# Two cross-attention blocks on one core: DMA queue entries placed by their producers, staging by chunks of heads, another order in the prologue and three banks at the end

## What is computed

```python
h1 = _ln(x, n1_g, n1_b)
x = _attn(h1, h1, q1, k1, v1, o1_w, o1_b, heads) + x
h2 = _ln(x, n2_g, n2_b)
x = _attn(h2, context, q2, k2, v2, o2_w, o2_b, heads) + x
h3 = _ln(x, n3_g, n3_b)
a, g = jnp.split(h3 @ ff_w1 + ff_b1, 2, axis=-1)
x = a * jax.nn.gelu(g, approximate=False) @ ff_w2 + ff_b2 + x
# _attn: softmax(q k^T / 4) v per head, then @ wo + bo
```

## Time and profile before

| what | value |
|---|---|
| median of three runs | 3865.36 us (3864.6 to 3879.61) |
| the profiled execution's own time | 3857.31 us |
| its span | 3855.5 us |
| mean granted TensorE clock | 0.914 of full speed |
| PE busy | 3224.7 us, 84% |
| weight loads (PEld) | 1495.8 us, 39% |
| DVE busy | 2090.1 us, 54% |
| ACT busy | 1996.1 us, 52% |
| POOL busy | 624.3 us, 16% |
| DMA engines, mean share of queue q1 | 33.7% |

### The profile page before, as it was taken

One profiled execution on the slowest core, in us unless ns is written; L12 is line 12 of the kernel. 1 busy time (PEld: TensorE's weight loads), 2 busy tenths in 40 slices (PEclk: granted clock), 3 DMA queues, 4 the chain that ended last, 5 costly groups with the idle time before them and its releaser, 6 DMA issues.

```text
span 3855.5 us, 43782 instructions
## 1 busy us (share of the span) xinstructions
PE 3224.7 (84%) x16320; PEld 1495.8 (39%) x16320; DVE 2090.1 (54%) x2565; ACT 1996.1 (52%) x3816; POOL 624.3 (16%) x676
## 2 busy tenths in 40 slices
PE   3686788899789878989889887898989979887867
PEld 1233343334344433534345332444334534533334
DVE  2554565667546655567546655555756645455410
ACT  1353366556555555556554565555655556454521
POOL 2113121212202121021201132021210031001010
PEclk9798898889899988999889998999989989998979
DMA  2642335431433344332333445333333133222202
GB/s 72 159 133 60 81 87 139 113 92 43 120 94 86 81 96 114 78 104 65 109 92 78 114 111 144 94 92 84 87 100 82 44 84 103 59 40 51 65 17 68
DMA packets 194323, 340.88 MB, mean 88 GB/s; under 512 B 19192, under 2 KB 101504, under 8 KB 192832
## 3 DMA queue, kind: packets, MB, share of 16 engines
q1 hardware_dynamic: 194112, 338.08, 33.7%
HBM read 202.29 MB, written 114.75 MB: 82 GB/s over the span
## 4 chain that ended last, share of the span: by engine, by line
PE 62%; DMA 11%; DVE 9%; ACT 6%; SPq 5%; issue 4%; POOL 3%; ACTq 0%; DVEq 0%; POOLq 0%
PE po L1053 12%; PE pr L1038 12%; PE pd L1019 8%; DVE mx L854 7%; DMA QS<-scr_q 6%; PE pf L969 5%; PE pf L977 5%; PE pf L916 4%; PE pf L957 3%; PE pf L939 3%; PE pf L948 3%; ACT ET L779 3%; DMA scr_k<-HS 2%; SPq L513 2%; PE pf L972 2%
## 5 line engine op out<-in xcount | busy, mean ns | idle before, releaser
L779 ACT ACTIVATE ET<-pr 128x512 f32<-128x512 f32 (+1 forms) x2720 | 1478.4, 597 | 1418.5 <-PE pr L1038 1406.0
L854 DVE TENSOR_REDUCE mx<-pd 128x2 f32<-128x804 f32 (+2 forms) x1600 | 1582.7, 1032 | 1056.2 <-PE pd L1019 1052.7
L1038 PE MATMUL pr<-QS,KS 64*128 64x512 f32 (+1 forms) x2720 | 877.1, 514 | 80.4 <-ACT ET L779 77.9
L1019 PE MATMUL pd<-KS,QS 64*128 64x400 f32 (+2 forms) x3200 | 636.4, 396 | 308.3 <-DMA QS<-scr_q 200.8
L1053 PE MATMUL po<-ET,V 128*32 128x512 f32 (+2 forms) x5440 | 779.9, 648 | 0.8 <-issue 0.6
L1038 PEld LDWEIGHTS pr<-QS,KS 64*128 64x128 f32 (+1 forms) x2720 | 345.3, 188 | 948.4 <-ACT ET L779 638.1
L1019 PEld LDWEIGHTS pd<-KS,QS 64*128 64x128 f32 x3200 | 374.4, 200 | 422.8 <-DMA QS<-scr_q 213.5
L673 POOL TENSOR_TENSOR HS<-uT,HS 128x512 fp32r<-128x512 f32 (+2 forms) x168 | 190.0, 1131 | 737.6 <-ACT uT L744 737.6
L969 PE MATMUL pf<-HS,WS 128*128 128x512 f32 x800 | 241.1, 433 | 72.2 <-DVE uT L847 24.9
L689 POOL TENSOR_TENSOR OA<-OA,DEN 128x512 f32<-128x512 f32 (+1 forms) x48 | 60.9, 1269 | 1311.4 <-DVE DEN L862 1311.4
L862 DVE RECIPROCAL DEN<-DEN 128x128 f32<-128x128 f32 (+1 forms) x192 | 170.5, 922 | 104.4 <-DMA DEN<-OU 103.7
(11 more groups left out here) (63 smaller groups left out, 2174.7 us busy)
## 6 DMA issues: line engine op xcount, KB each, us to landing
WS<-parts SPq DMA_DIRECT2D x160, 320.0 KB, 2.9
KS<-scr_k SPq DMA_DIRECT2D x80, 600.8 KB, 10.3
QS<-scr_q SPq DMA_DIRECT2D x80, 512.0 KB, 10.6
scr_k<-HS SPq DMA_DIRECT2D x144, 200.0 KB
scr_q<-HS SPq DMA_DIRECT2D x96, 256.0 KB
KS<-scr_k SPq DMA_DIRECT2D x80, 192.0 KB, 3.6
scr_k<-HS SPq DMA_DIRECT2D x48, 256.0 KB
OA<-OU SPq DMA_DIRECT2D x320, 32.0 KB
```

The lines of the kernel that those rows point to most:

```text
L779: activation(ET[0:q.rows[k], s % 2, 2 * pair + e, :], pr[e][0:q.rows[k], :], ACT.Exp).then_inc(score_free, 1)
L854: v.reduce_max(mx[:, t, 2 * p:2 * p + 2, c], pd[no % 2][:, :, 0:cols], AX_X).then_inc(unit_free, 1)
L1019: ins = mm(pd[no % 2][:, e, 0:cols], queries[:, t * P:(t + 1) * P], keys, start=True, stop=True)
L1038: mm(pr[e][0:m, :], keys, queries, start=True, stop=True).then_inc(score_ready, 1)
```

## The change

- **SP.** `beside` is split in three: loads behind a fill stand 2 beats behind it (`LOAD`), stores behind a split 4 (`STORE`), the bias row 8 (`LOAD_ROW`). `move_rows` stands 8 beats behind a group's end instead of 6; inverts at 14 to 17 instead of 13 to 19, the multiplication at 18 instead of 20.
- **Staging.** `stage_group` waits only for the last store of the chunk of heads that its group reads (`split_for`); k2's jobs go chunk of heads by chunk. The first unit stands from `_at + 7` instead of `_at + 5`.
- **Prologue.** `BEFORE` holds only chunk 0 of q1 and k1; chunks 1 and 2 (four fills) go to beats 1 to 9. DVE's memsets of KS stand behind the first measure. k2 of pass 0 and q1, k1 of pass 2 are spread over later beats; v1 is placed and waited for tile by tile.
- **Phases.** Two v2a fills go ahead of t3, and four a fills instead of three go with gelu.
- **Layer norm.** POOL adds the four bias rows behind the last tile instead of one behind each.
- **End.** From o2 of pass 7 on, fills take turns in three banks (pf, pr0, pr1); n3 measures a tile as soon as its o2 is in; g is written with Gelu at once; X is stored by tiles.

```diff
+KEY_JOBS = [(c, n, cols) for c in range(KC) for n, cols in CHUNKS]
-        seq = (mixed(places("tc", 0), places("n1", 1)) + places("t1", 1) + places("q1", 1) + places("k1", 1)
-               + places("k2", 0))
+        seq = [p for f in range(1, KC) for p in (("q1", 0, f), ("k1", 0, f))]
+        seq += mixed(places("tc", 0, 0, 3), places("n1", 1)) + places("t1", 1)
+        seq += [p for f in range(KC) for p in (("q1", 1, f), ("k1", 1, f))]
+        seq += places("tc", 0, 3) + places("k2", 0, 0, len(CHUNKS))
...
+        behind = places("v2a", c + 1)
         if c:
-            first, rest = gate(c - 1, 3)
-            seq += places("t3", c - 1) + places("g", c - 1) + [first] + rest
-        behind = places("v2a", c + 1)
+            first, rest = gate(c - 1, 4)
+            seq += behind[:2] + places("t3", c - 1) + places("g", c - 1) + [first] + rest
+            behind = behind[2:]
...
-BEFORE = places("n1", 0) + places("t1", 0) + places("q1", 0) + places("k1", 0) + places("v1", 0)
+BEFORE = places("n1", 0) + places("t1", 0) + [("q1", 0, 0), ("k1", 0, 0)] + places("v1", 0)
...
-COPY, MOVE, INVERT, DIVIDE = 5, 6, (13, 15, 17, 19), 20
+COPY, MOVE, INVERT, DIVIDE = 5, 8, (14, 15, 16, 17), 18
+LOAD, STORE, LOAD_ROW = 2, 4, 8
...
-    _at = max(4 * _host.end if _host else FIRST_BEAT, _stored + 1 if _stored >= 0 else FIRST_BEAT)
+    _at = max(4 * _host.end if _host else FIRST_BEAT, _stored + STORE + 1 if _stored >= 0 else FIRST_BEAT)
-    _from = max(_at + 5, _free, 0)
+    _from = max(_at + 7, _free, 0)
...
-                for own, count in stored_through(max(SPLIT[k, q.i, STAGE[k] - 1] + 1 for k in kinds)):
+                for own, count in stored_through(SPLIT[split_for(q)] + 1):
                     sp.wait_ge(own, count)
...
-                for p in PLACES.get(beat, []):
-                    beside(*p)
+                for p in PLACES.get(beat - LOAD, []) if beat - LOAD >= 0 else []:
+                    loads_behind(*p)
+                for p in PLACES.get(beat - STORE, []) if beat - STORE >= 0 else []:
+                    stores_behind(*p)
+                for p in PLACES.get(beat - LOAD_ROW, []) if beat - LOAD_ROW >= 0 else []:
+                    row_behind(*p)
                 for q in STAGE_AT.get(beat, []):
                     stage_group(q)
...
-                pool.wait_ge(w_in["b"], LOADED["b", stage, i])
-                pool.wait_ge(norm_done, at + 1)
-                gp.tensor_tensor(X[:, b, t, :], X[:, b, t, :], brow[:, :], ALU.add).then_inc(bias_done, 1)
+                if t == TT - 1:
+                    pool.wait_ge(w_in["b"], LOADED["b", stage, i])
+                    pool.wait_ge(norm_done, at + 1)
+                    for k in range(TT):
+                        gp.tensor_tensor(X[:, b, k, :], X[:, b, k, :], brow[:, :], ALU.add).then_inc(bias_done, 1)
...
+        def bank(no):
+            return pf if no < TAIL else (pf, pr[0], pr[1])[(no - TAIL) % len(tail_free)]
...
                 if beat == FIRST_BEAT:
+                    set_key_rows()
                     for u in range(len(GROUPS[0].units)):
```

More of the change, by code:

```diff
@@ L246, with split_for @@
             _user = _p
+TAIL = FILL["o2", N - 1, 0]
+def split_for(q):
+    own = [("q" if x == "q" else "k") + ("1" if q.kind == "S" else "2") for x in "qk"]
+    fills = [(own[0], q.i, q.g // 2)]
+    if q.kind == "S":
+        fills.append((own[1], q.i, q.g // 2))
+    else:
+        fills.append((own[1], q.i, len(CHUNKS) * (q.g // 2 + 1) - 1))
+    return max(fills, key=lambda p: SPLIT[p])
 STAGE_AT, UNITS_AT, TURN_AT, = {}, [0] * BEATS, {}
@@ L413, in blocks_kernel @@
         fill_free = sem("fill_free")
+        tail_free = [sem(f"tail_free{i}") for i in range(3)]
         low_done = sem("low_done")
@@ L533, in beside, with stores_behind @@
                         load_chunk(cc)
+                if stage in ("g", "a") and chunk_no(stage, i, f) + 2 < (i + 1) * 2 * FM:
+                    load_chunk(chunk_no(stage, i, f) + 2)
+                if stage not in LN_STAGES:
+                    for which, what, l in LOAD_BEHIND.get((stage, i, f), []):
+                        sp.wait_ge(fill_ready, FILL[stage, i, f] + 1)
+                        load_weights(which, what, l)
+                if stage == "tc" and f == STAGE[stage] - 1 and i < 2:
+                    sp.wait_ge(fill_ready, filled(stage, i))
+                    load_context(i + 1)
+                if stage == "ff2":
+                    if f == TT - 1 and i + 3 < N:
+                        sp.wait_ge(fill_ready, filled(stage, i))
+                        load_context(i + 3)
+                    if i // B == L - 1:
+                        for own, count in freed_through(FILL[stage, i, f]):
+                            sp.wait_ge(own, count)
+                        sp.dma_start(out[i % B, f * P:(f + 1) * P, :], X[:, i % B, f, :]).then_inc(x_stored, 16)
+            def stores_behind(stage, i, f):
                 if stage in ("q1", "k1", "q2", "k2"):
                     store_split(stage, i, f)
-                if stage in ("g", "a") and chunk_no(stage, i, f) + 2 < (i + 1) * 2 * FM:
-                    load_chunk(chunk_no(stage, i, f) + 2)
                 if stage == "w" and f:
@@ L541, in beside, with row_behind @@
                     load_raw(i, f)
-                for which, what, l in LOAD_BEHIND.get((stage, i, f), []):
-                    if which == "b":
+            def row_behind(stage, i, f):
+                if stage in LN_STAGES:
+                    for which, what, l in LOAD_BEHIND.get((stage, i, f), []):
                         sp.wait_ge(bias_done, TT * (LN0[stage, i] + 1))
[L545 to L555, removed]
-                        sp.wait_ge(fill_free, filled(stage, i))
-                        sp.dma_start(out[i % B].rearrange("(t p) d -> p t d", p=P), X[:, i % B, :, :]
-                                     ).then_inc(x_stored, 16)
+                        load_weights(which, what, l)
             def stage_group(q):
@@ L825, in measure @@
                         dve.wait_ge(fill_free, filled("ff2", i - B))
-                elif t == 0:
-                    dve.wait_ge(fill_free, filled("o1" if stage == "n2" else "o2", i))
+                elif stage != "n1":
+                    for own, count in freed_through(FILL["o1" if stage == "n2" else "o2", i, t]):
+                        dve.wait_ge(own, count)
                 v.bn_stats(stats[:, t, :], X[:, b, t, :]).then_inc(stats_done, 1)
```

144 lines of the change are left out of this document (91 added, 53 removed).

## The result

The changed kernel took 3684.7 us, median of 4 runs (3679.0 to 3690.2), beside 3865.0 us for the kernel before: a ratio of 0.953, 95% interval 0.950 to 0.956. So it is faster by 4.5%, where 6.5% was forecast. The time lies in the range of 3515 to 3700, 73 us above the forecast; the profiled execution stands at 3690.1.

The account below looks back on a forecast made before the run. PE was taken to set the pace but to be stopped often, above all by staging. 3857.3 - 47.9 + 11.2 - 193 - 23 = 3604.6, plus 8.1 for the runs, said as 3612 us; range 3515 to 3700.

Parts of the forecast that it names:

- Prologue, -48: Before the first unit: DVE's first measure ahead of the memsets, bias rows later, four fills out; 47.9 us sooner, at 55.7.
- Rival 3: In the prologue, DVE's memsets hold POOL: last normalising ends at 46 instead of 21 us, +25, time 3638; chance 0.06.
- The fills come back, +11: The four fills taken from the prologue go to beats 1 to 9, 2.8 us of PE each: +11 us.
- Staging, -169 of stops: PE's stops at the staging of queries and keys: of 200.8 us, 169 go, with SP punctual and PE two beats later.
- New stops, +56: Stores and ff_w1 chunks now behind stagings stop ACT and soon PE: 56 us, bounds nothing and 110.
- Other stops, -45: PE's stops elsewhere: 20 us go at t3, 16 at ff_w1 chunks, 9 from DVE's wait for X.
- Times 1.22: Between first and last score, each us of PE stop costs 1.22 us of span: net 158 gives -193 us.
- 660 us at the lower level: Over the span, PE's granted clock of 0.914 was read as some 660 us at the lower of its two levels.
- The two pairs of the earlier trace: Stretches of the kernel before with the same matmuls (368, 397): 1.16 and 1.29 us of span per us of PE idleness.
- End, -23: From o2 on at the end: three banks, measuring ahead, g and a fills 2.7 us apart, X by tiles; 23 us less.
- rival 2: Stores behind stagings hold ACT: new stops at the upper bound 110, time 3679, ACT's store waits over 80 us; chance 0.22.

Follow-up runs that it names:

- the pair of kernels: The changed kernel (3696.2 us, run again) beside it with queue entries at their producers' beats and units five beats behind a staging (3801.1 us).
- Both undone: Changed kernel with loads, stores and bias rows at their fill's beat and units five beats behind a staging instead of seven: 3801.1 us, ratio 0.9848.
- no lags: Changed kernel with loads, stores and bias rows back at the beat of their fill (0, 0, 0): 3763.7 us, ratio 0.9757.

## Why the prediction was right in its sign and 73 us short

**Prologue, -48.** Right: the first exponential comes 51.2 us sooner (117.6 to 66.4), of which undoing the memsets returned 30.7 (29.4 by the prediction). Rival 3 is refuted: POOL's normalising, begun at 12.92 within the memset of 12.70, took its 1.44 us. The Trainium skill, SBUF — State Buffer, "SBUF: two separate sides", has DVE and GpSimd block each other for whole instructions when DVE is in a two-port mode or reads two SBUF inputs. A memset reads none, and the prediction took it for no two-port mode; the trace agrees, nothing is blocked.

**The fills come back, +11.** Not seen apart: the first two phases fell by 31 us together, and the third (0, 2) grew by 13.6; of the others only the last grew too, by 3.

**Staging, -169 of stops.** Right in its sum, by another path. Between first and last exponential 128.4 us went from the waits for QS and 41.3 from those put to issue, 169.7 together; the pair of kernels gives 169. But the prediction took all of it from the QS waits and expected 30 us of them to be left (7.8 before group 0, 6 before the last two passes, 18 in them); 71.5 were. The 7.8 and the 18 came true, 6.9 and 17.1. The 6 is the term that failed: 47.5 us in sixteen stops of 0.9 to 4.9, because SP is not at the staging when the host ends, as the text had it, but 4 to 8 us late at fourteen places. Its own issuing of the stores ahead has a good part in that, which the text had read as waits for ACT and POOL.

**New stops, +56.** About right: 63 by the pair, bounded rightly by 0 and 110. But only part of it is what the prediction named. ACT's waits for its stores are 41.5 us in all, as the text said (24.5 scr_q, 17.0 scr_k), but they were 33.6 before, so 8 are new; PE's for ACT ahead of k2's fills grew 13 to 19. A third, 21 to 23 us, is a wait that no term held: units that start two beats later have less room, and PE waits for DVE's maxima between them, 232 times where it was 126. A fourth is no wait at all and is missing in the sum: the 18 to 27 us that the same spacing adds to PE's busy time ("Both undone").

**Other stops, -45.** This term failed by half or more. The gate's place is worth 22 us of PE's idle time, where t3 and the ff_w1 chunk had been put at 36; and DVE's wait for X, gone as foretold, gave nothing that can be seen. With 169.7 removed and 63 added, the 119.9 measured leave 13 for this term in the whole kernel. The likely step is the assumption that a wait of ACT or DVE (24.9 and 14.2 us in the earlier trace rows) is PE's wait at 0.6 to 0.8 of its size.

**Times 1.22.** This is the step that failed most. The net stops were to be 158 and are 119.9; at 1.22 they would still have given 146, and gave 90.5, with 11 of fills moved in. PE's busy time in the stretch rose by 29.4: 30.3 at full level (11 the moved fills, 19 the units' spacing) less 1 that the clock gave, where 0.22 x 158 = 35 had been put. Over the whole kernel the clock gave 7 us and the work at full level grew by 18, so that the span followed PE's idle time almost one to one, 167.2 for 177.6, by accident and not by a rule.

The reading "660 us at the lower level" missed what those 660 hold. PE was busy in 432 of them; after, there are 509, and it was busy in 417. So the change took away 151 us at the lower level, of which 137 were PE standing and only 15 PE working. About beat 636 it can be seen: before, the clock was low from 983.6 to 997.2 with PE standing until 993.4, so 3.8 us of work were slow; after, it was low from 918.9 to 925.7 with PE standing until 919.5, so 6.2 us were. The shorter stop has the longer slow stretch of work behind it.

Yet a price above one was not wrong in itself. The two pairs of the earlier trace rows gave 1.16 and 1.29; whole kernels with the units left in place give 1.46 (no lags) and 1.68 (stores two beats behind), the one with only the units' distance undone 1.18, the one with both 1.00. All are sums of the same three parts, idle time, work at full level, and half of the work at the lower level, and no fixed factor stands for them. Why the kernel before, with the most idleness of all, worked only 432 us at the lower level is open.

**End, -23.** 25.5 in the first profile, but 16 to 19 of the 147.7 before against the usual length of the other kernels; g's fills are 2.7 us apart, as foretold, and held by their loads.

The bounds that the text set for itself hold, the first two closely: the wait for QS is 71.5 (wrong would be over 80), the span 3688.3 (over 3700), the clock 0.931 where 0.95 was said. The measured time is near that of rival 2 (3679), yet rival 2's mark, ACT's waits for stores over 80 us, is not met (41.5). The profiled execution is 85 us above the 3604.6 of the sum for other reasons: no gain from the clock (34), other stops overrated (32), new ones underrated (7), the units' spacing in PE's busy time (19), less 7 that the prologue, the end and the staging gave beyond their terms.

In place of the sum, for the profiled execution: 51 from the prologue, 170 of staging stops less 63 that come back, 13 of other stops, 25 from the end, less 29 of busy time (11 the fills moved in, 19 the units' spacing, less 1 by the clock): 167.

## What to carry to other kernels

Don't multiply removed stops by a factor read from two stretches, or from one pair of kernels. Split the span into PE's idle time, its work at full level and its work at the lower level; only half of the last is what the clock can give back, and here PE worked in 432 of the 660 us at that level. Compare kernels in these three, or two of them may cancel, as 27 us of clock and 27 of work did here. When units or fills are moved to cover a wait, they are packed more closely somewhere: add the next engine's pace there as a term of its own, and what PE loses when its work falls into more pieces. And a single queue hands its lateness on: entries moved forward to save one waiter were paid by the waiters of the entries that they passed, here 38 us against 36, while entries put later, behind their producers, gained 51 to 68.

## What was not expected of the hardware

The stops put to issue before the first units of C groups are there when units stand five beats behind a staging (41.7 us before, 43.6 in the kernel with both covers undone, 38.5 with the units alone) and gone at seven (0.4, and 4.3 without the lags). They belong to that distance; what they are the profile doesn't tell, and it was not tried.

SP's own time for a store is uneven. In the changed kernel the median of 504 is 0.57 us, but one in seven takes over 1.1. Above, four of the six took 0.57 to 0.69 and two 1.5 and 1.6, and the bias row 1.25; at beat 840 six stores of k1 took 7.7 us with no wait for a producer. Such a row of stores ahead of a staging is enough to make it late. What makes some slow is not shown.
